# Two transformer layers in one kernel: the router in layer 1's late slots, other places of the turn for shared products, and four token buffers

## The reference

```
xn = layernorm(x)
x  = x + attention0(xn) + ffn0(xn)      # ffn0: gate, silu(gate) * up, down;
                                        # inputs and weights of each product in blockwise FP4
xn = layernorm(x)
x  = x + attention1(xn) + ffn1(xn)      # attention1 with biases
```

```
logits = relu(xf @ Wr1 + br1) @ Wr2 + br2
gates  = softmax(logits)
tg, ti = top_k(gates, 2);  tg = softmax(tg / 2)
out    = silu(xf @ Ws1 + bs1) @ Ws2 + bs2
for e in range(8):
    h   = silu(xf @ We1[e] + be1[e]) @ We2[e] + be2[e]
    out = out + sum(tg * (ti == e)) * h
```

## Time and profile before

| | us |
|---|---|
| median of three runs (1329.68 to 1333.38) | 1332.75 |
| the profiled execution | 1326.96 |
| its span, from the first to the last instruction | 1325.1 |
| PE busy | 1102.7 (83%) |
| DVE busy | 919.5 (69%) |
| ACT busy | 802.8 (61%) |
| POOL busy | 511.4 (39%) |

### The profile page before, as it was taken

One profiled execution on the slowest core, in us unless ns is written; L12 is line 12 of the kernel. 1 busy time (PEld: TensorE's weight loads), 2 busy tenths in 40 slices (PEclk: granted clock), 3 DMA queues, 4 the chain that ended last, 5 costly groups with the idle time before them and its releaser, 6 DMA issues.

```text
span 1325.1 us, 19383 instructions
## 1 busy us (share of the span) xinstructions
PE 1102.7 (83%) x6711; PEld 498.8 (38%) x6711; DVE 919.5 (69%) x1555; ACT 802.8 (61%) x1079; POOL 511.4 (39%) x514
## 2 busy tenths in 40 slices
PE   2678688888998898888888988898889866899995
PEld 1213323323432343234323432343234335788841
DVE  7878577877778877877788868786876222555633
ACT  1255376676776767676767676757676762333364
POOL 8641364244434443344335432541232241344420
PEclk9779789999999999999999999999999887999987
DMA  5622066116411741163127313611331256666763
GB/s 139 157 65 55 18 169 170 37 33 183 133 38 37 188 124 37 54 182 113 37 76 183 90 37 100 188 53 37 110 75 35 72 158 189 171 203 195 216 175 100
DMA packets 149633, 146.73 MB, mean 111 GB/s; under 512 B 13696, under 2 KB 142016, under 8 KB 149536
## 3 DMA queue, kind: packets, MB, share of 16 engines
q1 hardware_dynamic: 144048, 135.58, 37.2%
q0 software_dynamic: 4544, 9.38, 2.1%
q10 hardware_dynamic: 944, 0.54, 0.2%
HBM read 92.80 MB, written 52.12 MB: 109 GB/s over the span
## 4 chain that ended last, share of the span: by engine, by line
PE 41%; ACT 18%; DVE 17%; issue 7%; DVEq 5%; SPq 4%; DMA 3%; POOL 2%; ACTq 0%; POOLq 0%
DVE nm L1060 10%; ACT ex L772 9%; PE sums L393 8%; PE mx L405 7%; PE mx L490 5%; PE mx L499 5%; PE mx L374 5%; ACT L748 4%; PE ring L295 2%; PE ring L305 2%; PE ring L474 2%; SPq L1652 2%; DVEq L1010 1%; DMA scratch<-parts 1%; DMA rest<-parts 1%
## 5 line engine op out<-in xcount | busy, mean ns | idle before, releaser
L1060 DVE TENSOR_REDUCE nm<-mx 128x2 f32<-128x1024 f32 x512 | 601.1, 1216 | 102.4 <-PE mx L374 100.9
L772 ACT ACTIVATE ex<-mx 128x1024 f32<-128x1024 f32 x512 | 510.7, 1024 | 262.7 <-PE mx L405 262.4
L405 PE MATMUL mx<-qs,ks 128*128 128x512 bf16 (+1 forms) x1024 | 299.0, 391 | 37.1 <-ACT ex L772 11.3
L393 PE MATMUL sums<-ex,vs 128*18 128x512 f32 x2048 | 283.0, 612 | 4.4 <-ACT ex L772 1.7
L374 PE MATMUL mx<-km,qm 32*128 32x512 bf16 x1024 | 152.0, 397 | 63.4 <-DVE nm L1060 31.4
L405 PEld LDWEIGHTS mx<-qs,ks 128*128 128x128 bf16 (+1 forms) x1024 | 77.0, 98 | 308.9 <-ACT ex L772 129.8
L1500 POOL TENSOR_SCALAR binade<-binade 128x704 f32<-128x704 f32 (+1 forms) x24 | 57.0, 2376 | 251.7 <-DVE binade L1011 251.7
L374 PEld LDWEIGHTS mx<-km,qm 32*128 32x128 bf16 x1024 | 39.0, 91 | 216.5 <-issue 75.6
L1537 POOL DMA_INDIRECT xsort<-xn,pos_i x64 | 62.7, 979 | 76.6 <-DVE pos_i L1132 59.4
L1453 POOL TENSOR_TENSOR rstd<-veps,minus_half 128x4 f32<-128x4 f32 x16 | 16.7, 1046 | 182.9 <-DVE veps L970 182.9
L748 ACT ACT_TABLE_LOAD x64 | 82.1, 1283 | 1.2
(11 more groups left out here) (218 smaller groups left out, 1549.1 us busy)
## 6 DMA issues: line engine op xcount, KB each, us to landing
scratch<-parts SPq DMA_DIRECT2D x128, 256.0 KB, 3.7
ks<-scratch SPq DMA_DIRECT2D x64, 256.0 KB
qs<-scratch SPq DMA_DIRECT2D x64, 256.0 KB
qs<-wmoe SPq DMA_DIRECT2D x20, 578.0 KB, 4.0
ks<-wmoe SPq DMA_DIRECT2D x19, 578.0 KB, 3.8
qm<-scratch SPq DMA_DIRECT2D x64, 128.0 KB, 2.6
km<-scratch SPq DMA_DIRECT2D x64, 128.0 KB, 2.6
rest<-parts SPq DMA_DIRECT2D x32, 128.0 KB
```

The source lines that it names most:

```text
L393: done = pe.matmul(acc[32 * j:32 * j + 2 * VW, :], values[:, start:start + 2 * VW], ex[:, s % NEX, j, :], start=q == 0 and t == 0, stop=q ...
L405: done = pe.matmul(bank[:, j, :], ks[l][r, h, t * P:(t + 1) * P], qs[l][r, h, :], start=True, stop=True)
L772: act.activation(ex[:, s % NEX, 2 * i:2 * i + 2, :], bank[:, :, :], ACT.Exp, scale=SCALE).then_inc(free, 1)
L1060: dve.tensor_reduce(nm[l][:, t, h:h + 2], bank[:, :, :], AX.X, ALU.max, negate=True).then_inc(free, 1)
```

## The change

`router_hidden`, `router_logits`, `router_sort` and `router_exp` of a batch below 7 go from slots 1 to 4 of turn A(b+1) to slots 12 to 14 of turn B(b). In turn A `norm0` goes from (0, "b") to (0, "a"), `q0` and `k0` from (2, "a") and (3, "a") to (4, "d") and (6, "d") (for b = 1 from (5, "a") and (6, "a") to (5, "d") and (7, "d")), `v1` from (8, "d") to (1, "d"), and the two halves of `shared_hidden` from (7, "b") and (8, "b") to (2, "d") and (3, "d"). `ranks`, `places`, `router_choice`, `gate_difference`, `router_weights` and the quantising of h go to other places as the diff shows, and POOL takes `router_hits` first. The token tiles get four buffers, and SP issues more fetches ahead of the stores of batch 7.

```diff
-NW, NRES = 4, 4
+NW, NX, NRES = 4, 4, 4
...
-        xg = [spare[i][:, 2 * WROW:2 * WROW + 2 * XW].rearrange("p (h c) -> p h c", c=XW) for i in range(2)]
+        xg = [spare[i // 2][:, 2 * WROW + i % 2 * 2 * XW:2 * WROW + (i % 2 + 1) * 2 * XW].rearrange("p (h c) -> p h c", c=XW) for i in range(NX)]
...
# PE
                 if 1 <= b < LAST:
-                    if at == (0, "b"):
+                    if at == (0, "a"):
                         norm0(b + 1)
-                    if at == (2 if b > 1 else 5, "a"):
+                    if at == (4 if b > 1 else 5, "d"):
                         q0(b + 1)
-                    if at == (3 if b > 1 else 6, "a"):
+                    if at == (6 if b > 1 else 7, "d"):
                         k0(b + 1)
...
-                    if at == (8, "d"):
+                    if at == (1, "d"):
                         v1(b - 1)
                     if b - 1 < LAST:
-                        if at == (1, "d"):
-                            router_hidden(b - 1)
-                        if at == (3, "d"):
-                            router_logits(b - 1)
-                        if at == (10, "a"):
+                        if at == (8, "a"):
                             ranks(b - 1)
-                    if at == (7, "b"):
+                    if at == (2, "d"):
                         shared_hidden(b - 1, 0)
-                    if at == (8, "b"):
+                    if at == (3, "d"):
                         shared_hidden(b - 1, 1)
...
+                    if at == (12, "a"):
+                        router_hidden(b)
+                    if at == (13, "a"):
+                        router_logits(b)
...
# ACT, beside the same moves
-                        if at == (4, "b"):
-                            router_exp(b - 1)
-                        if at == (9, "b"):
+                        if at == (8, "b"):
                             router_tanh(b - 1)
...
+                    if at == (14, "b"):
+                        router_exp(b)
...
# DVE, beside the same moves
-                    if at == (1, "m"):
+                    if at == (2, "m"):
                         quantize_h(b, 1, 0)
-                    if at == (2, "m"):
+                    if at == (2, "c"):
                         quantize_h(b, 1, 1)
-                    if at == (2, "c"):
+                    if at == (3, "m"):
                         quantize_h(b, 1, 2)
-                    if at == (5, "m"):
+                    if at == (3, "c"):
                         quantize_h(b, 1, 3)
...
-                        if at == (3, "d"):
-                            router_sort(b - 1)
-                        if at == (7, "m"):
+                        if at == (1, "m"):
                             router_choice(b - 1)
-                        if at == (7, "c"):
+                        if at == (6, "m"):
                             gate_difference(b - 1)
-                        if at == (10, "b"):
+                        if at == (8, "b"):
                             places(b - 1)
-                        if at == (11, "m"):
+                        if at == (10, "m"):
                             router_weights(b - 1)
...
+                    if at == (13, "a"):
+                        router_sort(b)
...
# POOL
-                if 1 < b < LAST:
+                if b >= 1:
+                    router_hits(b - 1)
+                round_h(b, 1)
+                if 1 <= b < LAST:
                     second_part(b + 1)
                     third_part(0, b + 1)
-                round_h(b, 1)
-                if b == 1:
-                    second_part(2)
-                    third_part(0, 2)
                 if b >= 1:
-                    router_hits(b - 1)
                     scatter(b - 1)
...
# SP
             def fetch_tokens(i):
                 first = sp.value_load(x_row[0:1, i:i + 1], min_val=0, max_val=ROWS - TS)
-                if i >= 2:
-                    sp.wait_ge(ring_full, ring.at(("T", i - 2))[1] + 1)
-                    sp.wait_ge(y_row_ready, i - 1)
+                if i >= NX:
+                    sp.wait_ge(ring_full, ring.at(("T", i - NX))[1] + 1)
+                    sp.wait_ge(y_row_ready, i - NX + 1)
...
-                    for i in range(2, AHEAD):
+                    for i in range(2, NX + 1):
                         fetch_tokens(i)
+                    fetch_weights(NW)
                 store_early(1, b)
                 load_max(1, b)
                 if b == LAST:
-                    fetch_tokens(AHEAD)
-                    fetch_weights(AHEAD)
+                    for i in (1, 2):
+                        fetch_tokens(NX + i)
+                        fetch_weights(NW + i)
                 store_late(1, b)
...
-            for i in range(AHEAD + 1, NTILE):
+            for i in range(NX + 3, NTILE):
```

More of the change, by code:

```diff
@@ L181, in two_layers @@
         wbuf = [spare[i // 2][:, i % 2 * WROW:(i % 2 + 1) * WROW] for i in range(NW)]
-        xg = [spare[i][:, 2 * WROW:2 * WROW + 2 * XW].rearrange("p (h c) -> p h c", c=XW) for i in range(2)]
-        xgT = [spare[i][:, 2 * WROW + 2 * XW:2 * WROW + 2 * XW + 2 * P] for i in range(2)]
-        yo = [spare[i][:, 2 * WROW + 2 * XW + 2 * P:2 * WROW + 2 * XW + 4 * P] for i in range(2)]
+        xg = [spare[i // 2][:, 2 * WROW + i % 2 * 2 * XW:2 * WROW + (i % 2 + 1) * 2 * XW].rearrange("p (h c) -> p h c", c=XW) for i in range(NX)]
+        behind_x = 2 * WROW + 4 * XW
+        xgT = [spare[i][:, behind_x:behind_x + 2 * P] for i in range(2)]
+        yo = [spare[i][:, behind_x + 2 * P:behind_x + 4 * P] for i in range(2)]
         hm = [work[:, 0:EC * TS].rearrange("p (c t) -> p c t", c=EC),
               h_sb[:, :, :].rearrange("p t f -> p (t f)")[:, 0:EC * TS].rearrange("p (c t) -> p c t", c=EC)]
-        over_tiles = [spare[i][:, 2 * WROW + 2 * XW + 4 * P:2 * WROW + 2 * XW + 4 * P + NTILE * E].rearrange("p (i e) -> p i e", e=E)
+        over_tiles = [spare[i][:, behind_x + 4 * P:behind_x + 4 * P + NTILE * E].rearrange("p (i e) -> p i e", e=E)
                       for i in range(2)]
@@ L227, in two_layers @@
         w_in = [sem(f"w_in{i}") for i in range(NW)]
-        xg_in = [sem(f"xg_in{i}") for i in range(2)]
+        xg_in = [sem(f"xg_in{i}") for i in range(NX)]
         y_out = [sem("y_out0"), sem("y_out1")]
@@ L478, in tile_in @@
             def tile_in(i):
-                pe.wait_ge(xg_in[i % 2], (i // 2 + 1) * 16)
+                pe.wait_ge(xg_in[i % NX], (i // NX + 1) * 16)
                 bank = to_ring(("T", i))
                 for h in range(2):
-                    done = pe.transpose(bank[:, h * P:(h + 1) * P], xg[i % 2][:, h, 0:P], ident[:, :])
+                    done = pe.transpose(bank[:, h * P:(h + 1) * P], xg[i % NX][:, h, 0:P], ident[:, :])
                 done.then_inc(ring_full, 1)
@@ L1209, in tile_in @@
                 dve.tensor_copy(xgT[i % 2], bank[:, 0:TS]).then_inc(ring_free, 1)
-                dve.tensor_scalar(plane[i % 2][:, :], xg[i % 2][:, :, P + 1], t_exp[:, i:i + 1], float(PLANE), ALU.not_equal, ALU.mult)
-                dve.scalar_tensor_tensor(no_token[i % 2][:, :], xg[i % 2][:, :, P], 0.0, aside[:, i, :], ALU.is_equal, ALU.mult)
+                dve.tensor_scalar(plane[i % 2][:, :], xg[i % NX][:, :, P + 1], t_exp[:, i:i + 1], float(PLANE), ALU.not_equal, ALU.mult)
+                dve.scalar_tensor_tensor(no_token[i % 2][:, :], xg[i % NX][:, :, P], 0.0, aside[:, i, :], ALU.is_equal, ALU.mult)
                 dve.drain()
-                dve.tensor_tensor(plane[i % 2][:, :], plane[i % 2][:, :], xg[i % 2][:, :, P], ALU.add)
+                dve.tensor_tensor(plane[i % 2][:, :], plane[i % 2][:, :], xg[i % NX][:, :, P], ALU.add)
                 dve.drain()
@@ L1684, in fetch_tokens @@
                 first = sp.value_load(x_row[0:1, i:i + 1], min_val=0, max_val=ROWS - TS)
-                if i >= 2:
-                    sp.wait_ge(ring_full, ring.at(("T", i - 2))[1] + 1)
-                    sp.wait_ge(y_row_ready, i - 1)
-                sp.dma_start(xg[i % 2], xsort[bass.ds(first, TS), :].rearrange("(h p) c -> p h c", p=P)).then_inc(xg_in[i % 2], 16)
+                if i >= NX:
+                    sp.wait_ge(ring_full, ring.at(("T", i - NX))[1] + 1)
+                    sp.wait_ge(y_row_ready, i - NX + 1)
+                sp.dma_start(xg[i % NX], xsort[bass.ds(first, TS), :].rearrange("(h p) c -> p h c", p=P)).then_inc(xg_in[i % NX], 16)
             def store_base(b):
```

2 lines of the change are left out of this document (1 added, 1 removed).

## The result

The changed kernel takes 1341.18 us (median of seven runs, 1338.48 to 1346.76) against 1332.75 before (now also of seven runs, 1328.83 to 1336.04). The ratio is 1.0077, with a 95% interval from 1.0053 to 1.0100: slower by 7 to 13 us, where I had forecast 1331 and no change. The profiled execution took 1341.18 with a span of 1339.5, which is 14.4 above the span of before; the profiled execution of before, 1326.96, was faster than all seven runs, and the runs on both sides spread over 7 to 8 us. So the two profiles show where the time went, and the ratio how much it is. The time lies inside my range, 1321 to 1342, but that is luck: its upper end stood for the clock in turn A, and the largest miss is in turn B.

What follows compares the result with a forecast made beforehand. Each slot has its own bound: PE (or PE and exponentials), ACT with shared products, or DVE in turn B. Terms 2.5 + 0.3 + 2.7 - 7.5 = -2.0 us put the median at 1331, range 1321 to 1342.

Steps and rivals of the forecast that it cites:

- Turn B's slots: Slots 12 to 14: router products run in idle time, the sort costs +0.9 us per turn B (bounds 0 and 1.8).
- The clock: Turn A's slots with shared pairs: one stretch of lowered PE clock per turn, 1.0 us (bounds 0 and 3.4).
- a sign of failure: The forecast would fail on the clock if slots 2 and 3 of turn A exceeded 8 us.
- the slower rival: Both shared-pair slots of turn A run at 1.2 GHz, 3.4 us per turn: +15, 1348 us; chance 0.24.
- My window for slot 9 of A(2): Slot after a shared pair took 4.39 us at clock 0.61, against 3.62 in A(4): 0.8 per slow stretch.
- Slots 0 to 4 and 6 to 11 of turn A: Moved products lengthen slots 2, 3, 4 and 6 and shorten 0, 7 and 8: -1.4 us a turn, to 66.2.
- the -1.4: Turn A(1) was taken to save the same 1.4 us as the later A turns, without new clock loss.
- The start of A(1): Batch 0's router delays the first score from 165.2 to 168.1, +3.2 us (bounds 0 and 4.5).
- The tiles: Expert tiles at the end: early fetches, and products moved into the stall before tiles 7 and 8, give -7.5 us.
- the 1.2 for the early fetches: Expert tiles: fetches issued ahead of the last stores gain 1.2 us (range 0 to 2.7).
- the rival that they bring nothing: SP stands on tile 2's read regardless, so tiles give -6.3, not -7.5: 1332 us; counted within the forecast's 0.40.
- The lower bound of 1114.1 for tokens(8): Tile 8's token fetch would come at 1114.1 to 1117.2, depending on whether a scatter again takes 7.0 us.

Runs made afterwards that it cites:

- h_before_maxima: The changed kernel with both shared pairs still in slots 2 and 3 of turn A, but ahead of the maxima (place b): 1327.73 us, 0.9951 to the kernel before.
- tiles_old: The changed kernel with two token buffers and SP's old order of fetches: ratio 1.0082 to the kernel before.

## Why the prediction was wrong

**Turn B's slots.** This is the step that failed most, in its sentence "router_sort stands on DVE itself ahead of slot 13's maxima and takes 577.78 to 578.68, 0.9". The length came from a place where POOL happened to be free of two-input work at that moment. In slot 13 POOL rounds h, and the sort takes 1.6. It then sets slot 14, with the lower clock behind it in some turns: +12.2 in six turns instead of 5.4. The row at 680.12 to 683.89, which I read for the room there, is slot 13 and not slot 12 as I called it, and it shows POOL busy for 3.69 of 3.77 us. The row that would have told was in the trace of before, as the same subtraction took 1.17 us in turn A(2):

```profile
318.53 1.17 DVE L1096 TENSOR_TENSOR le<-lsort 128x32 f32<-128x32 f32 x1
```

**The clock.** The place, the sign and, in A(2) to A(6), the size were right: these turns lose 5.5 us to it, 1.1 each, where 1.0 was forecast; A(2), at 8.4 in slot 3, passes the 8 us that I had set as a sign of failure. But A(1), which I exempted as being slow already, has a slot 3 of 8.5, 1.8 more than at full clock, and A(7) lost none. What was wrong is what I said against the slower rival, that PE's longer products cost only what they exceed ACT by. Behind the maxima they are in line with ACT, 1.4 less than the pair each time. The price of the place itself was in the sum: 0.6 a slot and the clock make 14.4 in seven turns, and h_before_maxima got back 14.7 by the profiles and 17 by the medians. My window for slot 9 of A(2) starts 0.9 too late; the slot takes 4.38, and the 0.8 stands.

**Slots 0 to 4 and 6 to 11 of turn A.** Most were right to 0.1 or 0.2. Slot 8 came out 0.3 shorter, but slots 1, 10 and 11 gave +0.1 in all and not -0.4, so at full clock a turn gained 1.0 and not 1.4. I also took A(4) for the turn. Its slot 2 is 4.8, but over A(2) to A(6) this slot is 3.7 to 4.8, as ACT waits there for the store of `parts` in some turns only; the mean turn before is 67.5 and not 67.6. With 0.5 more of clock and two single slots this makes +2.0 of -2.0. In A(1) the -1.4 had no ground at all: q0 and k0 stood in its slots 5 and 6, slots 2 and 3 took 1.95 and 3.82 and not 4.8, and the turn gave +1.7, 1.8 of it the clock. The gain comes from the router that left, 2.4 to 3.1 a turn, and the moves of q0, k0 and norm0, added to it, take 1.6 of it back.

**The start of A(1).** The products were right in sum (168.19 against 168.1), but r1 took 1.05 where I took 0.6, and the handoffs made up for it. The exp behind the sort on ACT was missing, some 0.25, and the score's own lower clock, some 0.4.

**The tiles.** T11 to T13 was near, 9.98 against 9.2. Tile 8 is no earlier than before, so the 1.2 for the early fetches is missing too; with that 0.8 it makes most of the step from -7.5 to -5.2. This fits the rival that they bring nothing, but tiles_old does not settle it. The lower bound of 1114.1 for tokens(8) does not follow from my rows: with 3.3 for 7.0 it is 1113.4.

By the table the forecast's -2.0 was a sum of +8.9 and -10.9. The profiles give 16.4 us more: 6.8 in the B turns, 4.0 in A(2) to A(6), 3.1 in A(1), 2.3 in the tiles and 0.9 at the start of A(1), less 0.7 in A(7). The B turns alone would have turned the sign.

## What to carry to other kernels

A duration holds for its neighbours as well as for its operands: before moving a small DVE row, look at what POOL does at the new place, and take the longest time that the same row has anywhere in the trace. In this kernel a product whose result ACT waits for belongs ahead of the work that fills PE, under the exponentials, where its own length reaches no one and the clock little. The length of a slot that is to be changed is best read in all turns, as a wait may stand in some of them alone. And a move that gains only because another one made room should be tried together with it and without it: the version with the lowest time keeps all the moves and mends two places.
